# First expert stage of a hybrid SSM, attention and mixture-of-experts block: one chunk dense, three chunks as sorted blocks

## What is computed

```python
x = x + ssm(LN(x))            # diagonal state space layer, D = 128
x = x + ffn(LN(x))            # 8 experts, the two best of each token
x = x + attention(LN(x))      # 16 heads of 64, 512 x 512 scores, a bias by relative position
x = x + ffn(LN(x))            # the same experts again

def ffn(x, router_w, w_gate, w_up, w_down):
    topk_vals, topk_idx = top_k(x @ router_w.T, 2)
    g = sigmoid(topk_vals); g = g / (g.sum(-1) + 1e-10)
    out = 0
    for e in range(8):        # w_gate[e], w_up[e]: 128 x 256, w_down[e]: 256 x 128
        ge = sum(where(topk_idx == e, g, 0))
        out = out + ge * ((silu(x @ w_gate[e]) * (x @ w_up[e])) @ w_down[e])
    return out
```

## Time and profile before

| | us |
|---|---|
| runs of the kernel before | 774.41, 772.56, 775.21 |
| their median | 774.41 |
| profiled execution, device time | 772.99 |
| its span, from first to last instruction | 771.2 |
| PE busy | 729.5 (95%) |
| DVE busy | 588.4 (76%) |
| ACT busy | 494.3 (64%) |
| POOL busy | 368.8 (48%) |
| attention begins (first scores) | 201.45 |
| second expert stage, first sorted transposes | 659.27 |

### The profile page before, as it was taken

The page is one execution under the profiler, slowest core; times in us unless marked ns, Lnnn a source line. Parts: engine busy times, 40 slices in busy tenths (PEclk is TensorE's granted clock), DMA queues, the critical chain, the costliest instruction groups (busy, mean ns, idle before and its releaser), DMA issues.

```text
span 771.2 us, 13934 instructions
## 1 busy us (share of the span) xinstructions
PE 729.5 (95%) x4314; PEld 508.1 (66%) x4314; DVE 588.4 (76%) x1659; ACT 494.3 (64%) x1149; POOL 368.8 (48%) x422
## 2 busy tenths in 40 slices
PE   4988899999779999999999999999999999998997
PEld 3666688787556666666566667567657566677785
DVE  7998777778699876776876767876798888477485
ACT  6457566664667776775775775776675686564554
POOL 1074899985344344343433442442445776504551
PEclk9999999999999999999999999999999999999999
DMA  9011484565000000000000000006000512032422
GB/s 243 4 41 33 87 134 97 84 194 227 1 2 1 0 2 1 1 1 1 1 2 1 1 2 1 1 24 159 2 1 18 154 49 79 18 90 70 121 77 56
DMA packets 52616, 40.15 MB, mean 52 GB/s; under 512 B 2993, under 2 KB 48433, under 8 KB 52545
## 3 DMA queue, kind: packets, MB, share of 16 engines
q1 hardware_dynamic: 50752, 35.57, 18.2%
q0 software_dynamic: 1792, 3.68, 1.7%
HBM read 29.98 MB, written 9.26 MB: 51 GB/s over the span
## 4 chain that ended last, share of the span: by engine, by line
PE 72%; DVE 18%; issue 5%; ACT 3%; POOL 2%; DMA 0%; DVEq 0%; ACTq 0%; POOLq 0%
PE psum L1415 14%; PE psum L1397 11%; PE psum L1382 11%; PE psum L310 8%; PE psum L312 6%; PE psum L311 6%; PE psum L578 4%; PE psum L1339 4%; DVE prob L1542 3%; PE psum L1075 3%; DVE ln_stats L325 2%; PE psum L1046 2%; POOL hid_lo L805 1%; DVE probT L1549 1%; DVE qkT_lo L1556 1%
## 5 line engine op out<-in xcount | busy, mean ns | idle before, releaser
L1872 POOL TENSOR_SCALAR prob<-prob,ones 128x512 f32<-128x512 f32 x256 | 174.0, 692 | 256.1 <-DVE ones L1531 255.8
L1766 ACT ACTIVATE prob<-prob,ones 128x512 f32<-128x512 f32 x256 | 183.6, 719 | 125.7 <-DVE ones L1542 125.7
L1542 DVE CUSTOM_DVE_ANT_0 prob<-psum,bias_band 128x512 f32<-128x512 f32 x256 | 161.5, 687 | 63.1 <-PE psum L1382 62.0
L1397 PE MATMUL psum<-ident,prob 128*128 128x128 f32 x1024 | 124.0, 273 | 1.3 <-DVE ones L1542 1.0
L1415 PE MATMUL psum<-probT,v 128*64 128x512 f32 x512 | 124.0, 605 | 0.0
L1397 PEld LDWEIGHTS psum<-ident,prob 128*128 128x128 f32 x1024 | 114.6, 141 | 11.9 <-issue 3.9
L805 POOL TENSOR_TENSOR hid_lo<-hid,hid_hi 128x512 fp32r<-128x512 f32 x64 | 94.4, 1494 | 35.4 <-ACT hid_hi L625 35.1
L1549 DVE COPY probT<-psum 128x512 f32<-128x512 f32 x128 | 82.1, 677 | 8.2 <-PE psum L1397 8.2
L1772 ACT COPY probT<-psum 128x512 f32<-128x512 f32 x128 | 74.1, 579 | 1.2 <-PE psum L1397 0.8
L1415 PEld LDWEIGHTS psum<-probT,v 128*64 128x64 f32 x512 | 31.0, 136 | 55.1 <-issue 54.2
L696 DVE TENSOR_TENSOR hid<-hid,gate_all 128x512 f32<-128x512 f32 x56 | 54.7, 982 | 8.9 <-DMA gate_all<-gates 2.6
(11 more groups left out here) (287 smaller groups left out, 1405.2 us busy)
## 6 DMA issues: line engine op xcount, KB each, us to landing
gate_all<-gates SPq DMA_DIRECT2D x28, 256.0 KB, 6.8
bias_band<-bias_rows SPq DMA_DIRECT2D x16, 448.0 KB, 9.0
ys<-y SPq DMA_DIRECT2D x8, 256.0 KB
xs<-x_norm SPq DMA_DIRECT2D x1, 1472.0 KB, 6.7
x_res<-in_x SPq DMA_DIRECT2D x4, 256.0 KB, 5.3
w_raw<-in_w_gate SPq DMA_DIRECT2D x8, 128.0 KB, 4.0
...
```

The lines of the kernel that those rows point to most:

```text
L1397: last = nc.tensor.transpose(bank[turned_home(n) + h][:, j * P:(j + 1) * P], prob[:, n % PROBS, h, j * P:(j + 1) * P], ident[:, :])
L1542: nc.vector.tensor_tensor_reduce(out=prob[:, buf, h, :], in0=bank[scores_home(n) + h][:, :], in1=row_bias, scale=-1.0, scalar=NEG_START, o ...
L1766: nc.scalar.activation(prob[:, buf, h, :], prob[:, buf, h, :], ACT.Exp, bias=peak[:, buf, h:h + 1], scale=-1.0, accum_out=total[:, buf, h: ...
L1872: nc.gpsimd.tensor_scalar(prob[:, buf, h, :], prob[:, buf, h, :], inv[:, buf, h:h + 1], 1.0, ALU.mult, ALU.mult).then_inc(a_n, 1)
```

## The change

The first expert stage keeps the dense form for chunk 0 only. Chunks 1, and 2 and 3, become two new sorted groups (15 and 23 blocks), run with the functions of the second stage. The groups of the second stage keep their sizes and become 2, 3 and 4. The new pieces:

```diff
-        GROUPS = [(0, 2 * QT), (2 * QT, 3 * QT), (3 * QT, 4 * QT)]
+        GROUPS = [(QT, 2 * QT), (2 * QT, 4 * QT), (0, 2 * QT), (2 * QT, 3 * QT), (3 * QT, 4 * QT)]
+        STAGE = [0, 0, 1, 1, 1]
```

```diff
+        def dense_down(pe, e):
+            pe.wait_ge(DN["mul"], 2 * e + 2)
...
+            for n in range(QT):
+                for h in range(MT):
+                    last = nc.tensor.matmul(bank[DY_BANK + e % 2][:, n * P:(n + 1) * P],
+                                            d_hid[:, e % 2, h, n * P:(n + 1) * P],
+                                            ws_down[0][:, e * MT * D + h * D:e * MT * D + (h + 1) * D], start=(h == 0),
+                                            stop=(h == MT - 1))
+            last.then_inc(DN["dn"], 1)
...
+        def dense_add(dve, e):
+            dve.wait_ge(DN["dn"], e + 1)
...
+            for n in range(QT):
+                last = nc.vector.scalar_tensor_tensor(out=x[:, n, :], in0=bank[DY_BANK + e % 2][:, n * P:(n + 1) * P],
+                                                      scalar=dense_tile("gates")[:, n, e:e + 1], in1=x[:, n, :],
+                                                      op0=ALU.mult, op1=ALU.add)
+            last.then_inc(DN["add"], 1)
```

```diff
+        def blocks_first_pool(pool):
...
+            for i in range(2 * QT):
+                third_of_step(3 * 4 + i)
+                scatter_rows(pool, 0, i // 2, i % 2)
+            for i in range(4 * QT):
+                if i < 3:
+                    third_of_step(3 * 7 + i)
+                else:
+                    pool.wait_ge(GS["gu"], i - 2)
+                scatter_rows(pool, 1, i // 2, i % 2)
+            for i in range(2 * QT):
+                pool.wait_ge(GS["gu"], 21 + i)
+                gather_rows(pool, 0, i // 2, i % 2)
...
+                if n < 4 * QT:
+                    gather_rows(pool, 1, n // 2, n % 2)
```

The bias comes in five parts, since rows of the new groups lie in its home:

```diff
+            load_sorted(0)
+            sp.wait_ge(DN["dn"], E)
+            load_band(0)
+            load_sorted(1)
+            for q in range(Q1):
+                store_quad(sp, q)
+            sp.wait_ge(GS["dn"], B1)
+            sp.wait_ge(GS["ex"], 2)
+            load_band(1)
+            load_band(2)
+            sp.wait_ge(GS["yd"][1], 16 * (Q1 - QUADS_TO[0]))
+            load_band(3)
+            sp.wait_ge(GS["cb"], 3 * 2 * QT)
+            load_band(4)
```

1213 lines of the change are left out of this document (523 added, 690 removed).

## The result

| | before | after |
|---|---|---|
| device time, median (runs) | 774.81 (774.41, 772.56, 775.21, 776.55) | 782.58 (782.12 to 783.27, 4 runs) |
| profiled execution, its span | 772.99, 771.2 | 782.12, 780.3 |
| mean granted clock of that span | 0.999 | 0.967 |
| first scores of attention | 201.45 | 199.30 |

The ratio is 1.0103, with a 95% interval of 1.0075 to 1.0131: the change made the kernel 1% slower, where the forecast was 760 us (0.982) with a range of 745 to 772. PE is busy 707.7 us instead of 729.5, DVE 550.7 instead of 588.4. All engines do less, and the end comes later.

The account below looks back on a forecast made before the run. It took TensorE (PE) to bound the first expert stage and attention. Terms -26.5 + 6.5 + 3 + 3 = -14 from the profiled 772.99 gave 759, and 760 us with the runs' median 1.4 higher; range 745 to 772.

Parts of the forecast that it names:

- waits in the dense part: First expert stage: PE waits 4.7 and 6.2 us before chunk 2's and 3's transposes, 2.7 for group 1's count; 13.6 together.
- wait for the load, and for the block table: Between the block groups: PE idles 11 us for group 1's sorted load, bounds 8 to 14, then 2 for its block table.
- bias wait at slot 24: Attention's first batch: part 4 of the bias lands 7.5 to 8 us after issue, delaying scores 6.5; bounds 3 and 8.
- what attention's first batch gives back from there: Losses set against the 26.5 gain: bias load 6.5, DVE's extra work 3, TensorE's speed after idling 3.
- TensorE's speed after idling: Slower matmuls after PE's waits: 3 us charged for all the waits together, bounds 0 and 6.
- Rival C: TensorE slow after each of four long waits, 3 us each, 12 in place of 3: 769 us, chance 0.16.
- the signs of being wrong: First scores before 170 or after 185, first batch over 125 us, matmuls 0.43 apart behind waits, DVE operations 2 us and more.
- 103 + 57.7 + 13 + 3.6: First scores at 177.5: dense part ends at 103, then blocks and transpositions 57.7, load and block-table waits 13, projections 3.6.
- DVE's added work: Attention's first batch: 9.5 us more for DVE (combine products, norms, small operations, gates), taken to cost 3; bounds 0 and 8.
- Rival B: Attention's first batch becomes bound by DVE, whose added operations and POOL's wait each other out in slots 4 to 24: 776, chance 0.10.
- the rule on two inputs: Shared port pair: a two-input DVE operation and a GpSimd one reading there exclude each other for a whole instruction.
- Rival A: The waits are small, 8 and 8 in place of 13.6 and 11, with no clock loss: 745 us, chance 0.18.

Follow-up runs that it names:

- e10_busy_all: Changed kernel with matmuls whose result nobody reads put in front of six of PE's waits, nothing moved: 768.11 us.
- e5_pool: Changed kernel with one POOL wait added, holding its splits of expert weights until DVE has finished its last SSM product: 770.63 us.
- e1_busy: Changed kernel with matmuls whose result nobody reads put in front of four of PE's waits, nothing moved: 772.53 us.
- e3: Changed kernel with POOL issuing group 1's scatters without the pacing by blocks: 784.36 us.
- e9: e7 plus POOL's splits held until DVE's SSM chain is through, unpaced group 1 scatters, and sorted load ahead of the bias: 756.3 us.
- e6: Changed kernel with unpaced group 1 scatters and group 1's sorted load issued ahead of the first part of the bias: 768.78 us.
- e12: Changed kernel with 24 tiny ACT instructions put in front: 782.04 us.
- e13: Changed kernel with 24 tiny DVE instructions put in front: 781.31 us.
- e7: Changed kernel with dense-part work reordered on PE, DVE and ACT, chunk 3's combine earlier, group 1's first transposes later, its block table earlier: 746.39 us.

## Why the prediction was wrong

It had the places and lengths of the long waits right, and it failed in one term above all. From the profile of after against its own steps:

| step | predicted | measured |
|---|---|---|
| first dense matmul | 47.8 (46.0 and the logits) | 50.87 |
| waits in the dense part | 4.7, 6.2, 2.7 | 3.93, 5.56, 3.66 |
| chunk 0's last down ends | 103 | 117.1 |
| wait for the load, and for the block table | 11, 2 | 10.72, 2.52 |
| first scores | 177.5 | 199.30 |
| bias wait at slot 24 | 6.5 of 7.5 to 8 | 6.05 of DVE, 3.69 of PE |
| lead over the kernel before at the second scores | 26.5 | 4.8 |
| what attention's first batch gives back from there | 6.5 + 3 + 3 = 12.5 | 15.3 |
| all | -14 | +9.1 (spans) |

**The step that failed** is "TensorE's speed after idling ... I take 3 for all the waits together; bounds 0 and 6", together with its reading of the 13.6 and 11 us of waits as their whole cost. The rows that it had from the start of the kernel were the right ones; they were charged once, for a stage that has four long waits and several short ones. With the waits filled and everything else left, the same kernel is 12.3 us faster (e10_busy_all). In the rows of the changed kernel the half rate costs about 13 us ahead of the first scores alone: 1.7 at the start, 7.4 in the dense part, 3.8 in the blocks, as added up below. Rival C had the mechanism and charged 3 us to each of four waits, 12 in place of 3: its 769 was low since it took the rest of the sum over. The prediction had also named the signs of being wrong that then came: first scores after 185, matmuls 0.43 us apart behind the waits, DVE operations of 2 us and more beside POOL's. The clock is not the whole miss: e10_busy_all, with most of it gone, stands at 768.11 and not at 760.

The 21.8 us by which the scores came late are made up so (the parts add to 22.0, since the prediction's 103 + 57.7 + 13 + 3.6 is 177.3 and not 177.5):
- **The start, 3.1.** The prediction has no step for POOL's wider splits. DVE's last two SSM operations took 4.29, against 3.20 before and 2.45 in e5_pool, and PE's product behind them starts at 45.64 instead of 44.16, 1.5 late. The rest, about 1.7, is half rate behind the wait of 2.37: 1.2 in that product and 0.5 in the logits. e5_pool, where DVE and POOL work apart and no half rate follows, gives 3.8 back. Shown.
- **The dense part, 66.2 against 55.25, 11 late.** The three waits come to 13.15, close to the 13.6. The half rate is the greater part. From the rows above, eight matmuls at 0.43 after the first wait and ten after the second, at 0.20 too much each, with their transposes at 0.4, are 2.0 and 2.4; after the third, 16 fp32 matmuls cost 1.7 more, and the count and the first matmuls after it about 1.3. That is 7.4. The remaining 3.5 to 4 are smaller waits (1.76 at 96.56, 0.60 at 83.69) and what the sum left out; I have no row for each.
- **The blocks, 82.2 against 74.3, 7.9 late.** Waits as predicted. A quad is four blocks with their transposes. From the first transposes of group 1 at 147.46 to the next at 158.10, the rows behind the 10.72 cost 2.1 us more than the same rows at full rate, and those behind the 2.52 cost 1.7 more, 3.8 together; e1_busy, which fills only the first of the two waits, takes 8.73 for this stretch instead of 10.64. About 4 are two quads that take longer. The PE timeline of after, at the starts of successive quads' transposes:

```profile
122.87 0.60 PE L721 MATMUL psum<-ident,sorted 128*128 128x128 f32 x4
130.35 0.49 PE L721 MATMUL psum<-ident,sorted 128*128 128x128 f32 x3
164.35 0.60 PE L721 MATMUL psum<-ident,sorted 128*128 128x128 f32 x4
170.23 0.60 PE L721 MATMUL psum<-ident,sorted 128*128 128x128 f32 x4
178.63 0.60 PE L721 MATMUL psum<-ident,sorted 128*128 128x128 f32 x4
```

A quad takes 170.23 - 164.35 = 5.88, but 7.48 from 122.87 and 8.40 from 170.23; a third, from 178.63, takes 6.50. The prediction had charged 6.05 for each, a little too much, and with that these parts come to about 7 of the 7.9. Both long ones lie beside POOL's indirect DMAs, and ACT stops in the first with no releaser of its own:

```profile
125.35 0.59 ACT L729 CAST sortedT_hi<-psum 128x512 fp32r<-128x512 f32 x1 [2.37 <-remote]
```

**Attention's first batch, 15.3 instead of 12.5.** The second scores and the first ones of the second batch, in the PE timeline of after and, for the latter, of before:

```profile
203.17 0.50 PE L1113 MATMUL psum<-qkT_hi 64*128 64x512 f32 x2 [0.61 <-ACT v L1583]
325.63 0.50 PE L1113 MATMUL psum<-qkT_hi 64*128 64x512 f32 x2
```
```profile
315.16 0.50 PE L1382 MATMUL psum<-qkT_hi 64*128 64x512 f32 x2
```

The lead of 207.99 - 203.17 = 4.8 has become a lag of 325.63 - 315.16 = 10.5. A lag of 7.3 arises at slot 24, where PE's wait is 3.69, with matmuls at half rate behind it, so the 6.5 given for the bias wait was near the total and not the wait. Another 3.8 arises around 270.46, where PE waits 1.98 for DVE's normed rows of a chunk and the clock from 270 to 275 is 0.66; no term had this. DVE's added work was sized well: over the whole batch it is busy 101.23 us against 89.90, 11.3 more, where 9.5 had been given.

**What was right.** The places and lengths of the long waits; the wait for the load; DVE's wait for the bias; later batches nearly as long as before, with the two kernels 10.5 us apart after the first batch and 11.4 at attention's last product with v. The last stage came out 2.3 shorter, which no term had. Rival B did not come: DVE is idle for 25 of the 126 us of the first batch, no operation that was added there took 3.9, and PE's losses are mainly its two waits for DVE, of 1.98 and 3.69, and the low clock (0.94). The row that the prediction set beside the rule on two inputs, L336 with its 1.87 us, is an operation with one input, so it was no case of that rule; the two DVE rows of e5_pool and after are nearer to one. Rival A needed short waits, and they came at full length.

**What stays open.** Why ACT and DVE stop for 2 to 5 us beside POOL's runs of indirect DMAs in some kernels (changed, e3, e9) and not in e6, whose scatters follow each other as closely. Bias loads are not needed for it (the first two stops of e9), and a shift of ACT's or DVE's stream by 24 instructions changes nothing (e12, e13). And why the POOL wait gains 10 us alone and costs 10 in e7: in the traces 3.4 of the cost lie ahead of the scores, and some 4 of the gain are quads without a stop; for the rest there is no row. Small waits differ without an edit, too: PE's wait before expert 6 is 1.76 and 2.53 in the two traces of the changed kernel itself, and 0.97 in those of e5 and e6. So 1 to 3 us between single edits cannot be put down to the edit.
